# First attention of a macaron transformer kernel: scores made a second time with keys on partitions, so that exponentials are not transposed, and chunks overlap

## What is computed

```python
w = jnp.floor(MIN_W + (MAX_W - MIN_W) * scale).astype(jnp.int32)   # 24 to 120, from the data
half = w // 2                                                      # at most 60
q = (x @ Wq + bq).reshape(B, S, H, hd).transpose(0, 2, 1, 3)       # k and v alike
scores = jnp.einsum('bhqd,bhkd->bhqk', q, k) * inv_sqrt
band = jnp.abs(idx[:, None] - idx[None, :]) <= half
scores = jnp.where(band[None, None], scores, -1e+30)
attn = jax.nn.softmax(scores, axis=-1)
out = jnp.einsum('bhqk,bhkd->bhqd', attn, v)
out = jnp.einsum('bhqd,hdk->bhqk', out, W_o)
out = out.transpose(0, 2, 1, 3).reshape(B, S, D)
return out @ Wfc + bfc                                             # added to x
```

## Time and profile before

| | |
|---|---|
| median of three executions | 3266.82 us |
| the profiled execution, its own time | 3267.73 us |
| its span in the trace | 3265.8 us |
| TensorE matmul, busy | 2641.5 us (81%) |
| VectorE busy | 2432.7 us (74%) |
| ScalarE busy | 2312.6 us (71%) |
| GpSimd busy | 1636.1 us (50%) |
| A0, from its first instruction to its last | 426.9 to 943.3 us |

### The profile page before, as it was taken

How to read it: one execution, slowest core, us unless ns; L and a number is a source line. 1 busy time by engine, 2 the same in 40 slices (tenths; PEclk the granted TensorE clock), 3 DMA queues, 4 the chain that set the end, 5 groups by cost and what they waited for, 6 DMA issues and landing times. The chain is left out here.

```text
span 3265.8 us, 44956 instructions
## 1 busy us (share of the span) xinstructions
PE 2641.5 (81%) x13816; PEld 1818.6 (56%) x13818; DVE 2432.7 (74%) x4559; ACT 2312.6 (71%) x2789; POOL 1636.1 (50%) x1225
## 2 busy tenths in 40 slices
PE   4999958888859999399996587777777877549998
PEld 3877746666648777287774232232332322248887
DVE  5677757777756777688886787877878878378887
ACT  2555547676735555377772999999999999647776
POOL 2676620000026666454443666766767576444444
PEclk9999979898979999699997667676766676679999
DMA  3111100000001111211110000000000000021111
GB/s 111 52 52 39 39 1 2 0 0 0 0 28 52 52 39 39 79 52 40 52 39 0 0 1 1 1 1 1 1 1 1 1 1 1 0 92 52 52 39 51
DMA packets 13576, 86.60 MB, mean 27 GB/s; under 512 B 2176, under 2 KB 4224, under 8 KB 4224
## 3 DMA queue, kind: packets, MB, share of 16 engines
q1 hardware_dynamic: 13440, 84.96, 7.0%
HBM read 82.33 MB, written 2.62 MB: 26 GB/s over the span
## 5 line engine op out<-in xcount | busy, mean ns | idle before, releaser
L1648 POOL TENSOR_TENSOR A_Y<-A_Y,A_U 128x2048 f32<-128x2048 f32 x86 | 390.0, 4556 | 225.4 <-ACT A_U L1691 225.4
L1724 DVE TENSOR_SCALAR A_U<-ps 128x1024 f32<-128x1024 f32 x256 | 309.3, 1218 | 123.2 <-POOL A_Y L1648 59.3
L1730 DVE SCALAR_TENSOR_TENSOR A_U<-ps,A_U 128x1024 f32<-128x1024 f32 x256 | 311.3, 1216 | 55.6 <-PE ps L1860 55.6
L1860 PE MATMUL ps<-A_QT,A_KT 9*128 9x512 f32 x512 | 182.2, 707 | 194.2 <-DVE A_U L1730 160.9
L477 POOL TENSOR_TENSOR F0b_h<-F0b_h,dn 128x512 f32<-128x512 f32 x128 | 212.4, 1663 | 123.5 <-DVE F0b_h L408 123.3
L477 POOL TENSOR_TENSOR F0a_h<-F0a_h,dn 128x512 f32<-128x512 f32 x128 | 212.5, 1664 | 116.3 <-DVE F0a_h L408 116.1
L1860 PEld LDWEIGHTS ps<-A_QT,A_KT 9*128 9x128 f32 x512 | 66.3, 255 | 331.6 <-DVE A_U L1730 241.3
L1648 POOL TENSOR_TENSOR dn<-dn,A_U 128x2048 f32<-128x2048 f32 x42 | 190.3, 4551 | 112.1 <-ACT A_U L1691 112.1
L1691 ACT ACTIVATE A_U<-A_U 128x2048 f32<-128x2048 f32 (+1 forms) x96 | 236.5, 2464 | 0.0
L1832 PE MATMUL ps<-A_Y,A_VA 128*32 128x512 f32 x688 | 227.5, 795 | 5.8 <-DVE A_OT L1630 3.0
L1088 ACT ACTIVATE A_M<-A_M,A_nmax 128x192 f32<-128x192 f32 (+1 forms) x512 | 203.8, 471 | 34.0 <-DVE A_nmax L1203 32.3
(11 more groups left out here) (365 smaller groups left out, 8350.9 us busy)
## 6 DMA issues: line engine op xcount, KB each, us to landing
dn<-weight_rows SPq DMA_DIRECT2D x32, 1024.0 KB, 4.7
F1a_cwb<-weight_rows SPq DMA_DIRECT2D x16, 1024.0 KB, 4.6
F1b_cwb<-weight_rows SPq DMA_DIRECT2D x16, 1024.0 KB, 4.7
dn<-in_down SPq DMA_DIRECT2D x2, 2048.0 KB, 12.3
stage<-in_up SPq DMA_DIRECT2D x1, 2560.0 KB, 9.1
X<-in_x SPq DMA_DIRECT2D x1, 2048.0 KB, 8.2
F1a_h<-in_up SPq DMA_DIRECT2D x1, 2048.0 KB, 7.7
F1b_h<-in_up SPq DMA_DIRECT2D x1, 2048.0 KB, 7.8
```

Of the source, the lines that this page charges most:

```text
L1648: eng.tensor_tensor(flat(y_slot(m, h)), flat(y_slot(m, h)), flat(Um[:, h % UR]), ALU.add).then_inc(s["t_ready"], 1)
L1724: eng.tensor_scalar(u_step(n), d_pair(n), 0.0, None, ALU.max).then_inc(s["dp_vector"], 1)
L1730: eng.scalar_tensor_tensor(out=u, in0=g_pair(), scalar=CLAMP, in1=u, op0=ALU.min, op1=ALU.mult).then_inc(s["u_ready"], 1)
L1860: last = eng.matmul(ps[:, 4 + b, :], KT[r:r + 9, pair, kt * P:(kt + 1) * P], QT[r:r + 9, pair, :], start=True, stop=True)
```

## The change

- VectorE's mask and minimum step (`maxima`) works on the scores in place in PSUM and keeps only the minimum; it writes it straight into column 24 of that head's group in `QA`. `M`, the exponentials from SBUF and the transposes of exponentials are gone, and so are their copies.
- The column is turned together with q into `QM`, 25 rows; `KA` has a 1 in column 24. `shifted` makes the scores again with keys on partitions: first a matmul of the mask (`mask_b`, bf16, by the identity, 448 columns), then two 25-row matmuls added on it, which give score minus maximum plus mask. ScalarE takes one exponential over 448 columns straight from PSUM to `PT`.
- `outputs` takes key tiles whole, 192 or 256 queries at a time; V needs no half tiles.
- Work is by groups of four heads over all four tiles. q, k and q with its maximum are turned one group at a time between units, through one bank; copies are ScalarE's.
- q, k and v are projected in three steps inside the units before, one bank for all; GpSimd, not VectorE, lays out q and k and adds the output bias to x. `shifted` trails the scores by 7 units and `outputs` by 8, across the border of a chunk: no chunk has a head or an end of its own any more. The loop body is two chunks.

The diff, cut to its core:

```diff
-                QA = ab("QA", [P, TPC, H, 32], F32R)
+                QA = ab("QA", [P, 2, TPC, H, 32], F32R)
-                M = ab("M", [P, MR, 2, 2, WIN])
+                QM = ab("QM", [P, 2, S], F32R)
+                mask_b = ab("mask_b", [P, 2 * WIN], BF16)
...
                     @block.gpsimd
+                        def rows_q(k, p):
+                            q3 = qs[:, 0].rearrange("p t (h d) -> p (t h) d", d=HD)
+                            qa = QA[:, p]
+                            gate_gpsimd(eng)
+                            eng.tensor_copy(three(qa, 0), q3)
+                            eng.tensor_copy(three(qa, 1), q3)
+                            eng.drain()
+                            eng.tensor_tensor(three(qa, 2), q3, three(qa, 0).bitcast(F32), ALU.subtract)
+                            eng.drain().then_inc(s["asm_done"], 1)
...
                     @block.scalar
-                                    for b in range(2):
-                                        for r in range(2):
-                                            m = M[:, n % MR, b, r, w0:w1]
-                                            last = eng.activation(m, m, ACT.Exp, scale=-1.0,
-                                                                  bias=nmax[:, n % MR, b, r:r + 1])
+                        def take_turned(number, dst):
+                            eng.wait_ge(s["qk_tr"], number + 1)
+                            eng.activation(dst, ps[:, TURN, :], ACT.Copy).then_inc(s["taken"], 1)
+                        def weights(c, u):
+                            n, pair = UNITS * c + u, PAIRS * c + u // 2
+                            m2 = u // 2 % 2
+                            a, b = span(m2)
+                            for i in range(2):
+                                eng.wait_ge(s["s2_done"], 2 * n + i + 1)
+                                if not (isinstance(pair, int) and pair < 2):
+                                    eng.wait_ge(s["pv_done"], pair - 1)
+                                eng.activation(PT[:, m2, 2 * (u % 2) + i, a:b], ps[:, 4 + i, a:b],
+                                               ACT.Exp).then_inc(s["exp_done"], 1)
...
                     @block.vector
+                            for h in (2 * n, 2 * n + 1):
+                                g, t2, j = half_of(h)
+                                eng.wait_ge(s["sc_done"], c * HALVES + h + 1)
+                                for t in (2 * t2, 2 * t2 + 1):
+                                    _, _, w0, w1 = window(t)
+                                    part = ps[:, half_bank(h), (t % 2) * WIN + w0:(t % 2) * WIN + w1]
+                                    last = eng.tensor_tensor_reduce(
+                                        part, part, mask[:, w0:w1], -1.0, 3e38, ALU.add, ALU.min,
+                                        QA[:, p, t, 4 * g + j, 3 * HD:3 * HD + 1].bitcast(F32))
+                                last.then_inc(s["m_ready"], 1)
...
                     @block.tensor
+                        def scores(c, n, first):
+                            for h in (2 * n, 2 * n + 1):
+                                g, t2, j = half_of(h)
+                                if h >= 3:
+                                    eng.wait_ge(s["m_ready"], c * HALVES + h - 2)
+                                r = 32 * j
+                                for t in (2 * t2, 2 * t2 + 1):
+                                    lo, hi, w0, w1 = window(t)
+                                    last = eng.matmul(ps[:, half_bank(h), (t % 2) * WIN + w0:(t % 2) * WIN + w1],
+                                                      QT[r:r + 24, g % 2, t * P:(t + 1) * P],
+                                                      KT[r:r + 24, g, lo:hi], start=True, stop=True)
+                        def shifted(c, u, taken=None):
+                            g, m2 = u // 4, u // 2 % 2
+                            n = UNITS * c + u
+                            a, b = span(m2)
+                            for i in range(2):
+                                r = 32 * (2 * (u % 2) + i)
+                                if not (isinstance(n, int) and n == 0):
+                                    eng.wait_ge(s["exp_done"], 2 * n - 1 + i)
+                                eng.matmul(ps[:, 4 + i, a:b], ident_b[:, :], mask_b[:, a:b], start=True, stop=False,
+                                           skip_group_check=True)
+                                for m in (2 * m2, 2 * m2 + 1):
+                                    lo, hi, w0, w1 = window(m)
+                                    last = eng.matmul(ps[:, 4 + i, (m % 2) * WIN + w0:(m % 2) * WIN + w1],
+                                                      KT[r:r + 25, g, m * P:(m + 1) * P], QM[r:r + 25, g % 2, lo:hi],
+                                                      start=False, stop=True, skip_group_check=True)
+                                last.then_inc(s["s2_done"], 1)
+                        def outputs(c, p, u):
+                            if u % 2 == 0:
+                                return
+                            eng.wait_ge(s["exp_done"], 2 * n + 2)
+                            for m in (2 * m2, 2 * m2 + 1):
+                                for j in range(4):
+                                    last = eng.matmul(ps[32 * j:32 * j + 32, OUT0, lo:hi], VA[:, p, m, 4 * g + j, :],
+                                                      PT[:, m2, j, (m % 2) * WIN + w0:(m % 2) * WIN + w1],
+                                                      start=(m == 0), stop=(m == TPC - 1), skip_group_check=True)
...
+                            for n in range(UNITS):
+                                scores(c, n, first)
+                                v = n - LAST
+                                if v >= 0:
+                                    outputs(c, p, v)
+                                elif not first:
+                                    outputs(c - 1, 1 - p, v + UNITS)
+                                if n % 4 == 0:
+                                    turn(number, KA, (g + 1) % 4)
+                                if n % 4 == 1:
+                                    turn(number, QA[:, p if g < 3 else 1 - p], (g + 1) % 4)
+                                if n % 4 == 2:
+                                        turn(number, QA[:, p], g - 1)
+                                u = n - BEHIND
+                                if u >= 0:
+                                    shifted(c, u)
+                                elif not first:
+                                    shifted(c - 1, u + UNITS)
```

More of the change, by code:

```diff
@@ new lines, in _ @@
+                        all_chunks(eng, chunk)
+                        for n in range(LAST + 1):
+                            if n == 2:
+                                take_turned(2 + TURNED * B, QM[:, 1, :])
+                            if n == 3:
+                                copy_out(B - 1, 1, 2)
+                            if n < BEHIND:
+                                weights(B - 1, n + UNITS - BEHIND)
+                            if n == 2:
+                                norm_scalar(eng, s, B, B - 2, nxt, SPARE)
@@ new lines, in project, with turn @@
+                        def project(part):
+                            for t in range(TPC):
+                                last = eng.matmul(ps[:, SPARE, t * P:(t + 1) * P], xa[:, t * P:(t + 1) * P],
+                                                  qkv_w[lay][:, part * D:(part + 1) * D], start=True, stop=True)
+                            last.then_inc(s["pj_done"], 1)
+                        def turn(number, src, g):
+                            eng.wait_ge(s["taken"], number)
+                            for t in range(TPC):
+                                last = eng.transpose(
+                                    ps[:, TURN, t * P:(t + 1) * P],
+                                    src[:, t, 4 * g:4 * g + 4, :].rearrange("p h r -> p (h r)").bitcast(F32),
+                                    ident[:, :])
+                            last.then_inc(s["qk_tr"], 1)
@@ new lines, in _ @@
+                        all_chunks(eng, chunk)
+                        turn_out, turn_back, project_out = (tails[1][k] for k in (0, 2, 4))
+                        for n in range(LAST):
+                            outputs(B - 1, 1, n + UNITS - LAST)
+                            if n == 2:
+                                eng.wait_ge(s["m_ready"], B * HALVES)
+                                turn(2 + TURNED * B, QA[:, 1], 3)
+                            if n < BEHIND:
+                                shifted(B - 1, n + UNITS - BEHIND, 2 + TURNED * B + 1)
+                            if n == 2:
+                                eng.wait_ge(s["v_taken"], B + 1)
+                                eng.wait_ge(s["x_added"], B - 1)
+                                norm_turn_tensor(eng, s, B, SPARE)
+                            if n == 4:
```

(1 more changed line is left out.)

498 lines of the change are left out of this document (236 added, 262 removed).

## The result

The change made the kernel a little slower; 3233 us was forecast. The changed kernel took 3317.74 us, the median of 17 runs (3264.97 to 3379.13, and one of 5360.07), against 3267.14 us before (17 runs, 3260.92 to 3270.89). Taken again later, it was 3324.58 us (11 runs, 3268.25 to 3402.75). The ratio is 1.006 (95% interval 1.0033 to 1.0087), or 1.0054 (1.0029 to 1.008) the second time; it leaves out runs over 1.5% above the fastest, which here cuts off the kernel's own upper half, so that the medians (1.5% apart) say more than it does. Before, the runs lay within 10 us; now they scatter over more than 100.

What follows compares the result with a forecast made beforehand. No engine was full, TensorE nearest (47.9 of 58 us per chunk, clock 0.91). Chunks of 54 us plus the stage's ends gave 908.8 against 943.3, so 3267.7 - 34.5 = 3233 us; range 3165 to 3288.

Steps and rivals of the forecast that it cites:

- New waits: Prediction's step on TensorE's waits after the change: 1 us on 53, so 54 us per chunk at a clock of 1.00.
- rows 3: Profile rows before: TensorE held at the chunk's head by q and k copies, then the norm: 0.88, 1.17, 1.57 us.
- The stretch from 646 to 675 us: Part of a chunk before the change; clock 1.00 despite waits and changes of kind, cited against the clock rival.
- changes of kind: TensorE switching between strips, full-row work and outputs: 0.12 to 0.20 us each, 16.4 us per chunk after against 6.7.
- The clock does not come back: Rival: in every unit changes of kind keep TensorE's clock low; at 0.85 8 x 8 us added, 3300 us; chance 0.13.
- point of decision: Where the clock rival decides: 4.3 us more per chunk, 8 to 9 us of it at low clock, mean 0.92.
- TensorE's work per chunk: After the change: streams 36.5 us plus changes of kind 16.4, growing from 44 to 53 us.
- Waits for exponentials: Outputs wait for second scores' exponentials in units 1 and 15 only: 2 x 0.4, so 1 us per chunk.
- First scores at 451: Stage's start: scores at about 451 us instead of 457.42, 6 us earlier.
- bare load in the same strip: Rival: weight loads between same-strip matmuls not hidden, 6.4 us more per chunk, 51 in all, 3284 us; chance 0.05.
- Changes of kind are cheap here: Rival: mask-to-second-score loads run ahead, chunks 43 us instead of 54, 88 us more gained, 3145 us; chance 0.15.
- The sum: Stage's end: 451.1 + 8 x 54 + 5 + 4 - 4 + 20.7 = 908.8 against 943.3, 34.5 us less.

Runs made afterwards that it cites:

- e5: Changed kernel with the row range dropped, so second scores stream over all 128 rows, four heads summed (weights not attention's); 3156.58 us.
- e1: Changed kernel with both mask matmuls of a unit first, then its four second scores alternating between two strips; 3191.80 us.
- e2: Changed kernel with the mask matmuls left out, so exponentials are taken without the band; 3248.88 us.
- e3: Changed kernel with each mask matmul issued twice, the second overwriting the first with the same result; 3300.48 us.
- e8: e1 with each mask matmul issued twice, the second overwriting the first; 3227.07 us.
- e10: e1 with each second score issued twice into the same sum, so that scores are doubled; 3242.13 us.
- e6: e1 with ScalarE's exponentials of a unit moved ahead of its copy of turned rows; 3237.34 us.
- e7: e4 with ScalarE's exponentials of a unit moved ahead of the padded copies; 3215.29 us.
- e4: Changed kernel with second scores over all 128 rows, q zero-padded per head by four copies in place of one; 3256.11 us.
- e9: e4 with the four padded copies split in two halves, the first behind a unit's exponentials, the second heading the next unit; 3182.26 us.

## Why the prediction was wrong

**The step that failed** is the end of "New waits": "at a clock of 1.00, since no wait is near those of rows 3", with the reason given in the rival, that the clock "fell only behind waits of about a microsecond". It did so in the trace before. From that I took waits to be the only cause. In the changed kernel TensorE has almost none, and its clock is 0.80; of its falls, two came behind gaps of 1.9 and 2.0 us at the border of the loop body, which the list of waits did not foresee, and others, as that at 577 with 51 us at the low level, behind none. In e5 gaps of 2.25 and 2.52 us brought no fall. The stretch from 646 to 675 us, the evidence against the rival, was full of transposes of exponentials over 128 rows (128 per chunk, eight in a row). Those are just what the change removes; of the 36.5 us of streams that were left, scores over 24 and 25 rows were some 12 (5.3, and 32 x 0.21), where they had been 5.2 of 36.8. That this counts, no one run shows: e1 alone speaks for changes of kind, and e5 altered both. It follows from e2 (fewer changes of kind, lowest clock), e3 (as many, more 128-row streams, 0.92) and e8 beside e10 taken together. That the transposes themselves held the clock up was not tested; no run put them back.

**The rival that came true** is "The clock does not come back", given 0.13. Its price was right: it let 45 of 54 us double, which is 0.45 us for a microsecond at 1.2 GHz, and 0.44 was measured. Its point of decision was 8 to 9 us of low clock per chunk; the six chunks of the profiled run had 34 us each (2 x 0.19 x 61 for the first, and so on, 204 in all), and 51 + 0.44 x 34 = 66 us is their length. It reckoned with 0.85 and 3300 us; in the profiled run it was 3342. That the rival had the right price does not make its reason right: it gave the changes of kind as the cause, and only e1 bears that out in part. The median, 3317.74, lies 30 us above the range given, which ended with the milder forms of this rival.

**What held.**
- TensorE's work per chunk: 53 us forecast, 51 measured. The mask with two scores was to take 0.40 for streams, plus 0.20 and 0.16 for two changes of kind, 0.76; it takes 0.68. The streams are exactly 0.40 (e5), the changes 0.28.
- VectorE 32 forecast, 31.1 busy; ScalarE 29 forecast, 29.4; GpSimd under 12, 8.8 (all from the chunk at 708). In place, a mask step costs 0.04 us more. All of it stayed under TensorE, as said.
- Waits for exponentials: 1 us per chunk forecast, 4.7 us in six chunks measured, 0.8 each.
- First scores at 451 forecast, 449.91 measured.

**The other rivals.** A bare load in the same strip is out: two scores of 256 columns in one strip end 0.47 us after the first one's start, and one alone takes 0.38 to 0.39, so the second adds 0.09 and no load of 0.11 fits besides its stream. These ends are modelled; by starts, the chunk's work at full clock came 2 us under the forecast, where bare loads would have put it 6.4 over. The rule of the Trainium skill that stood behind this rival (page "TensorE: Matmul & The Clock Gate", section "Part 3: Packing small matmuls — row/col tiling") does not agree with the trace here. "Changes of kind are cheap here" is out too: it had 43 us per chunk, which is what e5 reaches when the changes are really gone. Without the low clock the profiled run would have been near 3197 us, 36 below the 3233 of the forecast: the clock, some 145 us, is more than the whole miss of 109. The sum was too high elsewhere, by 8 x 3 = 24 us in the chunks' work and the rest at the ends, where the rows of before had low clock in them (from 918 us on). These errors hid part of the miss; that is luck.

**What stays open.** Why the two profiles of the changed kernel part behind 714 us was not found, nor what starts a fall: several begin behind the router scores (eight matmuls of 8 columns in 1.06 us, L168) with no wait, and no run took these out. e6 beside e7 suggests that short waits count for more when the second scores are thin (0.83 with 21.7 us of waits, 0.93 with 35.3); how rows, waits and changes of kind add up can't be told from these runs. e1 differs from the changed kernel in clock and in work; of its 126 us gain 8 x 6 = 48 are work at full clock, and the rest is clock, but why exactly this order holds the clock (the same thin streams in less time, more of the time for the rest, and fewer changes of kind) was only argued. Whether it is the number of rows or the addressing in strips was not told apart: e4, e5, e7 and e9 changed both.

## What to carry to other kernels

Putting matmuls one after another into one strip of few rows saved no time here (0.68 us for a mask and two scores, 0.40 over all rows), and it went with a lower clock for everything around it: before a change takes 128-row work away, look at what kept the clock up in the stretch that is taken as evidence. Group matmuls of one kind (both masks, then all scores), since each pair of changes between strips and full rows cost 0.28 us here, and let matmuls in different strips alternate. If the operand can be padded with zeros at no cost on the path, all rows at once stream as fast as one strip does, without the changes of kind and at a higher clock (e9, 0.97). The copies for it cost 44.5 us of waits in e4, until they were split.

## What the runs showed that was not expected

- TensorE was busy for 50.00 of 50 us (changed kernel, 578 to 628) and for 150.66 of 153 us (e2, 653 to 806) with the clock at 1.2 GHz all the time. Being busy was not enough to bring it back.
- Issuing the mask twice (e3) raised the granted clock from 0.80 to 0.92, and 48 us more work did not lengthen the median (3300.48 against 3317.74 us); leaving it out (e2) lowered the clock to 0.59.
- Streaming 128 rows instead of 25, with the same instructions, took a chunk from 67.6 to 44.1 us (e5), some 7 of it (51 to 44) without the changes of kind and the rest by the clock.
- The changed kernel's runs scatter from 3265 to 3403 us, those of e5, at a clock of 1.00, over 8 us. A low clock alone does not do it: e6, at 0.83, stays within 7 us over its four runs.
